# Spreading a column over the partitions through DRAM: the second attention of a four-layer graph network

## The reference

```python
Xw = X @ Wv + bv
sj = Xw @ aw[:d, 0]
si = Xw @ aw[d:, 0]
e = leaky_relu(sj[:, None, :] + si[:, :, None] + ab[0], negative_slope=0.2)
alpha_matrix = A * jnp.exp(e)
transition = alpha_matrix / (jnp.sum(alpha_matrix, axis=-1, keepdims=True) + 1e-12)
for k in range(3):
    H = H + Xk @ Wk[k] + bk[k]
    Xk = jnp.einsum('bij,bjd->bid', transition, Xk)
return jax.nn.relu(H)
```

## Time and profile before

| | |
|---|---|
| median of 3 runs | 1489.31 us (1488.73 to 1489.68) |
| span of the profiled execution | 1487.0 us |
| TensorE busy | 1423.5 us, 96% |
| VectorE busy | 1206.8 us, 81% |
| ScalarE busy | 978.8 us, 66% |
| GpSimd busy | 949.7 us, 64% |
| mean granted clock of TensorE | 0.989 |
| data moved | 62.01 MB |

### The profile page before, as it was taken

How to read it: one execution, slowest core, us unless ns; L and a number is a source line. 1 busy time by engine, 2 the same in 40 slices (tenths; PEclk the granted TensorE clock), 3 DMA queues, 4 the chain that set the end, 5 groups by cost and what they waited for, 6 DMA issues and landing times.

```text
span 1487.0 us, 33717 instructions
## 1 busy us (share of the span) xinstructions
PE 1423.5 (96%) x8920; PEld 1263.7 (85%) x8920; DVE 1206.8 (81%) x4621; ACT 978.8 (66%) x2122; POOL 949.7 (64%) x974
## 2 busy tenths in 40 slices
PE   6799999999999999999999999999999999999975
PEld 5679988889888988988888988888988888988864
DVE  5778888888888888888888888888888888888773
ACT  4456667766667776667776666776666776666754
POOL 4555775666776666676666676675677666677524
PEclk9899999999999999999999999999999999999997
DMA  4001111101111110111110111110111110111001
GB/s 128 22 15 37 37 42 44 49 32 46 35 48 36 49 47 30 35 49 35 49 49 28 42 42 35 49 49 28 45 39 35 49 49 28 49 35 41 23 29 50
DMA packets 75372, 62.01 MB, mean 42 GB/s; under 512 B 3014, under 2 KB 70986, under 8 KB 75339
## 3 DMA queue, kind: packets, MB, share of 16 engines
q1 hardware_dynamic: 75338, 61.63, 12.7%
HBM read 36.45 MB, written 16.78 MB: 36 GB/s over the span
## 4 chain that ended last, share of the span: by engine, by line
PE 75%; ACT 11%; issue 5%; DVE 5%; DMA 1%; POOL 0%; DVEq 0%; ACTq 0%; POOLq 0%; SPq 0%
PE ps L343 35%; PE ps L347 18%; PE ps L328 16%; PE ps L491 4%; ACT wh L851 3%; ACT pT L940 3%; ACT h L918 2%; ACT h2T_hi L881 1%; ACT p L929 1%; PE ps L400 1%; ACT yT_hi L953 1%; DMA x_in<-in_x 1%; DVE stats L1329 1%; DVE h L1347 1%; DVE binc_T L1368 0%
## 5 line engine op out<-in xcount | busy, mean ns | idle before, releaser
L1130 POOL TENSOR_TENSOR x3n<-p,x 128x512 f32<-128x512 f32 x64 | 80.8, 1285 | 252.8 <-ACT p L929 252.8
L851 ACT ACTIVATE p<-ps,rs 128x512 f32<-128x512 f32 (+1 forms) x256 | 138.2, 582 | 106.4 <-PE ps L347 73.7
L1090 POOL TENSOR_TENSOR hT_lo<-hT,hT_hi 128x512 fp32r<-128x512 f32 x126 | 162.8, 1294 | 68.5 <-ACT hT_hi L871 65.4
L1085 POOL TENSOR_TENSOR rs<-var_e,neg_half 128x4 f32<-128x4 f32 x160 | 164.9, 1031 | 23.7
L343 PE MATMUL ps<-wl_hi,h2T_hi 128*128 128x258 f32 (+1 forms) x512 | 148.5, 371 | 7.8 <-ACT h2T_hi L881 7.2
L328 PE MATMUL ps<-p,alT 128*128 128x256 f32 (+1 forms) x512 | 136.9, 390 | 3.3 <-DVE h3T_lo L1239 2.3
L343 PE MATMUL ps<-wl_lo,h2T_hi 128*128 128x258 f32 (+1 forms) x512 | 132.9, 341 | 0.0
L347 PE MATMUL ps<-wl_hi,h2T_lo 128*128 128x258 f32 (+1 forms) x512 | 132.4, 340 | 0.0
L949 ACT ACTIVATE h3T_hi<-ps 128x512 fp32r<-128x512 f32 x64 | 38.0, 594 | 139.0 <-PE ps L491 138.9
L491 PE MATMUL ps<-ident,h 128*128 128x128 f32 x768 | 118.3, 278 | 9.9 <-DVE h L1347 9.4
L491 PEld LDWEIGHTS ps<-ident,h 128*128 128x128 f32 x768 | 92.3, 142 | 32.9 <-issue 10.4
(11 more groups left out here) (178 smaller groups left out, 4476.0 us busy)
## 6 DMA issues: line engine op xcount, KB each, us to landing
x_in<-in_x SPq DMA_DIRECT2D x32, 512.0 KB, 3.9
out_x<-x SPq DMA_DIRECT2D x32, 512.0 KB, 2.9
adj_f<-in_adjT SPq DMA_DIRECT2D x32, 256.0 KB, 2.9
adj_m<-in_adjT SPq DMA_DIRECT2D x32, 256.0 KB, 2.8
adj_l<-adj_m SPq DMA_DIRECT2D x32, 256.0 KB, 2.3
vqk<-in_l_wk SPq DMA_DIRECT2D x3, 256.0 KB, 5.2
x<-in_w2T SPq DMA_DIRECT2D x1, 512.0 KB, 5.1
x<-in_w1T SPq DMA_DIRECT2D x1, 512.0 KB, 5.9
```

What stands on the lines that cost most here:

```text
L851: return act.activation(dst, src, ACT.Copy, scale=scale)
L1085: pool.tensor_tensor(rs[:, layer, :], var_e[:, layer, :], neg_half[:], ALU.pow).then_inc(done, G)
L1090: pool.tensor_tensor(hTs[1][:, hc, :], hT[:, hc, :], hTs[0][:, hc, :], ALU.subtract).then_inc(S["hT_lo"], 1)
L1130: pool.tensor_tensor(x3n[:, s], p0[:, s], x2[:, s], ALU.add).then_inc(S["x3_ready"], 2)
```

## The change

`si` no longer goes through TensorE. SP waits for `sij`, stores the column of the four graphs to a small tensor in DRAM (2 KB), waits for that and loads it back broadcast to all 128 partitions, into `zb`. The leaky relu is done before the exponential: with s the full sum, 5 times leaky(s) is s + relu(4 s). ScalarE makes the relu into a new tile `ze` (`relu_edges`), GpSimd adds it to the spread column (`add_edges`), and ScalarE takes exp of 0.2 times that with `sjc[1]` as bias (`exp_edges`), in SBUF. VectorE's maximum is gone; `mid_columns` makes a third column `sjc[2]`, 4 times `sjc[0]`. On ScalarE the new steps stand behind `copy_h3T(0)`, with `copy_p10(1)` between them. `late_h3(1)` keeps its wait for `zb_ready`.

```diff
+STEEP = 1.0 / SLOPE - 1.0
...
+        si_row = nc.dram_tensor("si_row", [G, C, 1], F32).ap()
...
+                if r.has_mid:
+                    sp.wait_ge(S["sij_ready"], r.mid(G))
+                    sp.dma_start(si_row.rearrange("g c a -> c g a"), sij[:, :, 1:2],
+                                 allow_slow_non_contiguous=True).then_inc(S["si_stored"], 16)
+                    sp.wait_ge(S["si_stored"], r.loads(r.i - 1))
+                    sp.dma_start(zb[:], si_row.rearrange("g c a -> a g c").broadcast_to((P, G, C))).then_inc(S["b2_spread"], 16)
...
-                if r.has_mid:
-                    mid_b2(r)
...
-            def exp_edges(r, b):
+            def relu_edges(r):
                 act.wait_ge(S["sjc_ready"], r.mid(G))
-                act.wait_ge(S["b2_spread"], r.mid(G))
-                for g in (2 * b, 2 * b + 1):
-                    act.activation(zb[:, g, :], bank("b2")[:, g * C:(g + 1) * C], ACT.Exp, bias=sjc[:, 1, g:g + 1],
-                                   scale=SLOPE).then_inc(S["zb5_ready"], 1)
-                for g in (2 * b, 2 * b + 1):
-                    act.activation(bank("b2")[:, g * C:(g + 1) * C], bank("b2")[:, g * C:(g + 1) * C], ACT.Exp,
-                                   bias=sjc[:, 0, g:g + 1]).then_inc(S["eb_ready"], 1)
+                act.wait_ge(S["b2_spread"], r.loads(r.i - 1))
+                for g in range(G):
+                    act.activation(ze[:, g, :], zb[:, g, :], ACT.Relu, bias=sjc[:, 2, g:g + 1],
+                                   scale=STEEP).then_inc(S["eb_ready"], 1)
+
+            def exp_edges(r):
+                act.wait_ge(S["zb5_ready"], r.mid(G))
+                for g in range(G):
+                    act.activation(zb[:, g, :], zb[:, g, :], ACT.Exp, bias=sjc[:, 1, g:g + 1],
+                                   scale=SLOPE).then_inc(S["zb_ready"], 1)
...
-                    exp_edges(r, 0)
-                    exp_edges(r, 1)
                 if r.has_late:
                     copy_h3T(r, 0)
                 if r.has_mid:
+                    relu_edges(r)
                     copy_p10(r, 1)
+                    exp_edges(r)
                     copy_p10(r, 2)
...
+            def add_edges(r):
+                pool.wait_ge(S["eb_ready"], r.mid(G))
+                pool.tensor_tensor(zb[:], zb[:], ze[:], ALU.add).then_inc(S["zb5_ready"], G)
...
                 if r.has_mid:
+                    add_edges(r)
                     mask_edges(r)
...
+                dve.tensor_scalar(sjc[:, 2, :], sjc[:, 0, :], STEEP, None, ALU.mult, ALU.add,
+                                  accum_out=unread[:, 4, 2:3]).then_inc(S["sjc_ready"], G)
...
-            def mid_edges(r):
-                dve.wait_ge(S["zb5_ready"], r.mid(G))
-                dve.wait_ge(S["eb_ready"], r.mid(G))
-                dve.tensor_tensor(zb[:], bank("b2").rearrange("p (g c) -> p g c", g=G), zb[:],
-                                  ALU.max).then_inc(S["zb_ready"], G)
```

More of the change, by code:

```diff
@@ L175, in gnn_stack @@
         sij = sb("sij", G, 2)
-        sjc = sb("sjc", 2, G)
+        sjc = sb("sjc", 3, G)
         zb = sb("zb", G, C)
+        ze = sb("ze", G, C)
         alT = sb("alT", G, C)
@@ L228, in gnn_stack @@
         att_ready el_ready ea_ready x2_ready
-        st2 ag2 h2_ready var2 rs2_ready h2T_ready h2T_copied h2T_lo p2_ready p2_copied sij_ready sjc_a sjc_ready b2_spread zb_ready zb5_ready eb_ready al_ready
+        st2 ag2 h2_ready var2 rs2_ready h2T_ready h2T_copied h2T_lo p2_ready p2_copied sij_ready sjc_a sjc_b sjc_ready si_stored b2_spread zb_ready zb5_ready eb_ready al_ready
         p10_ready p10_copied ap_ready rsum_a rsum_ready z1_ready p0b_ready az_ready vb_ready relu_ready x3_ready x3_moved
@@ L236, in gnn_stack @@
         BANK = {"u": (0, 4, 3, 2), "y": (0, 7), "s": (4, 5), "d": (0,), "c2": (6, 5), "h1": (7, 1), "wh": (2, 3, 4,
-                5), "b1": (6,), "att": (1, 5), "h2": (4, 3), "p2": (4, 5, 6, 7), "p10": (7, 6, 7, 6), "b2": (5,),
+                5), "b1": (6,), "att": (1, 5), "h2": (4, 3), "p2": (4, 5, 6, 7), "p10": (7, 6, 7, 6),
                 "z": (1, 2, 3, 4), "ap": (0, 1, 2, 3), "az": (0, 3), "h3": (0, 5), "vqk": (4, 1, 6, 7), "ak": (6,),
@@ L535, in mid_p10 @@
                               0, (S["h2T_lo"], r.mid(2 * (g // 2) + 2))).then_inc(S["p10_ready"], 1)
-            def mid_b2(r):
-                pe.wait_ge(S["sij_ready"], r.mid(G))
-                wait(pe, S["p2_copied"], r.mid(2))
-                for g in range(G):
-                    last = spread(bank("b2")[:, g * C:(g + 1) * C], sij[:, g, 1:2])
-                last.then_inc(S["b2_spread"], G)
             def z_product(g):
@@ L1431, in mid_columns @@
                 dve.tensor_scalar(sjc[:, 1, :], sjc[:, 0, :], SLOPE, None, ALU.mult, ALU.add,
-                                  accum_out=unread[:, 4, 1:2]).then_inc(S["sjc_ready"], G)
-            def mid_edges(r):
-                dve.wait_ge(S["zb5_ready"], r.mid(G))
-                dve.wait_ge(S["eb_ready"], r.mid(G))
-                dve.tensor_tensor(zb[:], bank("b2").rearrange("p (g c) -> p g c", g=G), zb[:],
-                                  ALU.max).then_inc(S["zb_ready"], G)
+                                  accum_out=unread[:, 4, 1:2]).then_inc(S["sjc_b"], G)
+                dve.tensor_scalar(sjc[:, 2, :], sjc[:, 0, :], STEEP, None, ALU.mult, ALU.add,
+                                  accum_out=unread[:, 4, 2:3]).then_inc(S["sjc_ready"], G)
             def z1_scale(r):
@@ L1613, in body @@
                     late_ln3(r)
-                if r.has_mid:
-                    mid_edges(r)
                 if not r.steady and r.i == 0:
```

## The result

| | before | after |
|---|---|---|
| median | 1489.02 us (1488.49 to 1489.68) | 1887.18 us (1884.93 to 1890.25) |
| ratio after to before, 95% interval | | 1.2676 (1.266 to 1.2691) |
| span of the profiled execution | 1487.0 us | 1888.4 us |
| TensorE busy | 1423.5 us, 96% | 1531.9 us, 81% |
| mean granted clock of TensorE | 0.989 | 0.884 |

The changed kernel is 27% slower. The direction was forecast; the time, 1737 us and at most 1790, was not. The page of the kernel after, in the same order of reading as before: the busy table (to be laid beside the earlier trace rows), the clock in 40 slices, and two parts of the chain that ended last (its shares by engine, then by line). The last two rows are of the DMA issues.

A forecast was written before the change was run, and what follows sets the result against it. TensorE, busy 96% of the span, was taken to bound the kernel. Span 1487.0 + 168 for three waits (saved transposes included) + 80 for the clock + 2.3 gave 1737 us, range 1645 to 1790.

The forecast's parts named there:

- The two DMAs: SP's store and load back behind `sij`: 2.9 and 2.8 us, landing at 785.2, 2.5 us early and hidden.
- The late rival: Store of 5.8 and load of 3.9 us make the spread late: 1783 us, or 1830 at 3 us late; chance 0.13.
- Where ScalarE can begin: On ScalarE the relus stand behind `copy_h3T(0)` and start at 787.74; this order, not the DMAs, sets the start.
- The chain behind the relus: Relus, GpSimd's add, exponentials, mask, `rsqrt(4)` and first `z`, from 787.74 to `mid_ap(1)` at 795.1.
- 168 us for the three waits: TensorE waits at `late_h3(1)`, `mid_ap(0)` and `mid_ap(1)`: 5.4 us a round, 162 for thirty, 3 each for first and last.
- The clock, 80 us: TensorE falls to half clock in nearly every round, losing 2.6 us each over 31 rounds.
- What the change takes from TensorE, and the form on the other engines: Four transposes in `mid_b2` go, 0.37 us a round, 12 in all; VectorE's lost maximum and added column operation cost nothing.
- The sum: Whole kernel: span 1487.0 + 168 waits + 80 clock + 2.3 from span to median = 1737 us, 17% slower.

The follow-up runs named there:

- the packed column: The changed kernel with `sij` turned around, the column stored as 128 pieces of 16 B and `zb` holding the graphs interleaved: 1760.96 us, ratio 1.182.
- the kernel of the repair: The changed kernel with 16 B store pieces, relus before `copy_h3T(0)`, halved add, exponentials and mask, earlier `rsqrt(4)`, `late_h3(1)` not awaiting `zb_ready`: 1505.11 us, ratio 1.011.

## Why the prediction was wrong, point by point

- **The two DMAs: wrong, and the step that failed.** The prediction took 2.9 us for the store from a DMA of as many but larger pieces, 5.8 as upper end, and 2.8 and 3.9 for the load. Measured: 8.0 to 10.7 and 4.7 (median). The spread was to be there 5.9 us behind `sij`, 2.5 us before ScalarE was ready, and so to cost nothing. In the round shown the first relu starts after 12.7 us, when the spread is there; ScalarE was ready after 8.5. The late rival had the mechanism, but its range ended at 3 us late, and the relus were late by 5.0 us on average. Its price of 1 us a round for each us was a little low: 159.6 us of lateness cost 179, since the low clock lasts longer, too. The other forms of the store show what the nearest row, the output store, could not: it has as many pieces, but larger ones. The prediction also cites the Trainium skill, page "DMA: Bandwidth & Descriptors": one descriptor per element for a strided last dimension ("Rules for kernel authors"), and read-modify-write below 512 B ("Specifications"). The first agrees with the packets: 20421 under 512 B here, 8133 with the packed column, a difference of 32 x 384. The second is not shown by any run: 512 pieces of 4 B at 64 B cost 1.9 us and 128 of 16 B cost 1.4, so being under 512 B alone is cheap here. The fixed 2.0 us of the Trainium skill (same page, "Anatomy of one DMA") would have given an estimated 4 us for both, a third of what was measured.
- **Where ScalarE can begin: right as a bound, not the one that held.** In the round shown `copy_h3T(0)` starts at 986.80 and ScalarE is free from 987.40; the relus start at 991.65 behind the DMA. In the kernel without the store it held: 3.32 us of idle time for `late_h3(1)` against 3.3.
- **The chain behind the relus: right.** From the first relu to `mid_ap(1)` it was to take 7.36 us (787.74 to 795.1) and takes 7.48 (991.65 to 999.13), through the same five hand-overs.
- **168 us for the three waits: right.** With all three filled and the clock up, the kernel without the store is 171 us slower than the one before.
- **The clock, 80 us: wrong size.** It was to be 2.6 us a round and is 48 / 31 = 1.6. The fall itself came as forecast, from full clock (2.4 GHz) to 0.50 (1.2 GHz). In the kernel without the store:

```profile
902.00:903.00 1.00, 0.00 (x0) 1.00 0.00 0
903.00:904.00 1.00, 0.07 (x1) 0.98 0.00 0
904.00:905.00 1.00, 1.00 (x4) 0.50 0.00 0
...
910.00:911.00 1.00, 1.00 (x4) 0.60 0.00 0
911.00:912.00 1.00, 1.00 (x7) 1.00 0.00 0
```

  The clock is low from about 903.9 to 910.8, 6.9 us. But until 907.28 TensorE still waits for the mask and for `z`, which come from other engines and don't get later when it is slow: `mid_ap(1)` starts 8.65 us behind `late_h3(0)` here (898.63 to 907.28), and 8.72 in a round of the kernel with all waits filled, at full clock (872.04 to 880.76). Only the 3.5 us from the start of `mid_ap(1)` on should cost anything, and half of those is 1.8 us, near the 1.6 measured. The kernel with the longest wait filled bears that out: its low stretch is shorter by half, all of it behind the last wait, and its time is the same within 4 us. The prediction halved the whole low stretch; its three rows of 4.40, 6.00 and 5.25 us were stretches of unbroken work, and this one is not. The page "TensorE: Matmul & The Clock Gate" of the Trainium skill ("Part 1: The HAM clock gate") puts the ramp under 1% of a typical kernel. Here it is 48 of 1708 us, 2.8%, since it is paid 31 times, so the 15 us that the prediction worked out from that figure were too few.
- **What the change takes from TensorE, and the form on the other engines: right.** Costed at nothing beyond 0.37 us a round, 12 us in all; in the kernel of the repair TensorE is busy for 1423.5 - 1412.6 = 10.9 us less than before. The form alone with TensorE's spread is no slower.
- **The sum, made again from what was measured:** 1489.3 + 171 (three waits) + 48 (clock) + 152 (wait for the exponentials, by the late DMAs) + 5 (wait for the mask) + 24 (more of the lower clock, after a longer wait) = 1889, against 1887. Without the DMAs' error the forecast would have been too high, by 1737 - 1708 = 29, all of it the clock's.
- **What stays open.** Why many small writes close together report so late while their packets are over within a microsecond, and why the load then waits until some 10.7 us have passed since the issue of the store; why the report comes late in nine of 32 rounds (the packed store has nine, too, at 2.0 to 2.5 us in place of 1.4); and whether touching or crowding is what counts. The runs show when it happens, not by what.

## What to carry to other kernels

A small DMA is not priced by its bytes or its packets alone: ask how small its pieces are and how close together they land, and give it larger pieces (four floats side by side were enough here) or more room between them, before it becomes the link between two engines. When a step is moved onto an engine with a fixed order, look first at what that engine will be waiting for just ahead of it; here half of the chain ahead of that wait gained 53 us of 219 and the whole of it 208, with the data there early. And a stall of TensorE can cost more than its length (48 us here for a stretch with 5 us of waits a round; with waits of 1 us the clock stayed at 0.987); but count the low clock only over the work behind the last wait.

## What the runs showed of the hardware

- A store of 2 KB to DRAM, from one instruction on SP's queue, took 8.0 to 10.7 us as 512 touching floats, 2.7 (median) as 512 floats 16 B apart, 1.9 at 64 B apart, 1.4 as 128 pieces of 16 B, and 1.2 to 1.3 as four pieces of 512 B.
- The load that broadcasts 2 KB to 128 partitions landed after 3.1 us behind the large pieces, 3.7 to 3.9 behind those of 16 B, and 4.7 behind the touching floats.
- From the issue of the store to the first packets of the load that reads it back there were 10.4 to 11.7 us with the touching floats (median 10.7), 2.4 to 3.4 with pieces of 16 B (3.1), and 2.1 to 2.4 with four pieces (2.1).
- ScalarE took 0.51 us for 128 x 128 floats read at a stride of 16 B and 0.39 for contiguous ones; four in a row 1.74 to 1.76 and 1.28.
- Filling only the longest of three waits did not keep the clock (it fell later in the round, its mean rose from 0.927 to 0.958, and 1708 us became 1704). Filling all three did (0.987), and gave 48 us.
